# An attention-like mixer and a mixture of experts on one core: sixteen slots, tile steps laced with the mixer's last three steps, setup and scaling moved

## What is computed

```python
h = layernorm(x) * (1 + ca) + sa                      # sa, ca, ga, sb, cb, gb from silu(c) @ wmod, per batch
xi = silu(h @ Win + bin_)                             # 256 columns
# scan over the 512 tokens: state = 0.9 * state + xt * Bp; y = state . Cp + Dp * xt
x = x + ga * (y @ Wout + bout)
h = layernorm(x) * (1 + cb) + sb
p = softmax(h @ Wr + br); probs, idx = top_k(p, 2)    # 8 experts, two per token, renormalised
h_e = layernorm(relu(h @ W1[e] + b1[e]), g1, be1)     # 512 columns
y_e = layernorm(relu(h_e @ W2[e] + b2[e]), g2, be2)   # 128 columns
x = x + gb * sum over the two experts of gate * y_e
```

## Time and profile before

| | |
|---|---|
| median of 3 runs | 551.77 us (550.8 to 551.81) |
| the profiled execution | 549.6 us, its span 547.8 us |
| PE busy (matmuls) | 489.3 us, 89% of the span |
| DVE busy | 472.3 us, 86% |
| ACT busy | 400.9 us, 73% |
| POOL busy | 384.5 us, 70% |
| mean granted clock of PE | 0.969 |

### The profile page before, as it was taken

How to read it: one execution, slowest core, us unless ns; L and a number is a source line. 1 busy time by engine, 2 the same in 40 slices (tenths; PEclk the granted TensorE clock), 3 DMA queues, 4 the chain that set the end, 5 groups by cost and what they waited for, 6 DMA issues and landing times. The chain is left out here.

```text
span 547.8 us, 15172 instructions
## 1 busy us (share of the span) xinstructions
PE 489.3 (89%) x3075; PEld 389.0 (71%) x3075; DVE 472.3 (86%) x2217; ACT 400.9 (73%) x1107; POOL 384.5 (70%) x524
## 2 busy tenths in 40 slices
PE   2698897989896589899999999999999999999863
PEld 2264554555554469699999999999989899889740
DVE  5968899898988578598888899999999899999896
ACT  1435877587876357688888888888888798888763
POOL 4361477777777777866665668888888788769683
PEclk9999999999999589999999999999999999999996
DMA  6962011451111165454555555666666766666665
GB/s 176 309 186 77 31 54 50 95 111 54 55 50 54 55 174 134 136 151 138 143 146 145 173 144 177 179 187 161 182 186 151 181 193 159 184 182 195 189 180 154
DMA packets 79342, 77.81 MB, mean 142 GB/s; under 512 B 11086, under 2 KB 72681, under 8 KB 79126
## 3 DMA queue, kind: packets, MB, share of 16 engines
q1 hardware_dynamic: 70838, 59.92, 42.0%
q0 software_dynamic: 8416, 16.93, 8.7%
HBM read 54.65 MB, written 22.59 MB: 141 GB/s over the span
## 5 line engine op out<-in xcount | busy, mean ns | idle before, releaser
L577 POOL DMA_INDIRECT expert_results<-y,target x135 | 136.3, 1010 | 42.3 <-issue 41.0
L546 POOL DMA_INDIRECT expert_rows<-rows_ring,slot x128 | 123.4, 964 | 54.8 <-issue 53.6
L1344 PE MATMUL bank<-W,h2T 128*128 x1080 | 142.7, 275 | 0.7 <-ACT h2T L727 0.7
L1344 PEld LDWEIGHTS bank<-W,h2T 128*128 128x128 f32 x1080 | 131.2, 192 | 0.9 <-issue 0.9
L719 ACT ACTIVATE h1T<-bank 128x512 f32<-128x512 f32 x135 | 80.7, 598 | 44.6 <-PE bank L1329 43.6
L1108 DVE BATCH_NORM_STATS2 stf<-h1T 128x6 f32<-128x512 f32 x135 | 90.9, 673 | 0.0
L1335 PE MATMUL bank<-ident,h1T 128*128 128x128 f32 x540 | 80.9, 272 | 0.0
L1335 PEld LDWEIGHTS bank<-ident,h1T 128*128 128x128 f32 x540 | 67.3, 141 | 18.2
L727 ACT ACTIVATE h2T<-bank 128x512 f32<-128x512 f32 x135 | 79.6, 589 | 0.0
L1326 PE MATMUL bank<-b_parts,onesr 128*128 x135 | 65.3, 484 | 3.2 <-DVE h3lo L1100 3.2
L1084 DVE SCALAR_TENSOR_TENSOR wmod<-bank,rse,shifts 128x128 f32<-128x128 f32 x135 | 46.5, 344 | 20.5 <-PE bank L1344 7.1
(11 more groups left out here) (212 smaller groups left out, 1037.7 us busy)
## 6 DMA issues: line engine op xcount, KB each, us to landing
shifts<-expert_shifts SPq DMA_DIRECT2D x135, 192.0 KB
hrow<-expert_rows SPq DMA_DIRECT2D x135, 65.0 KB
xi<-expert_results SPq DMA_DIRECT2D x12, 512.0 KB, 5.1
X<-in_L_attn_x SPq DMA_DIRECT2D x8, 512.0 KB, 7.1
out_x<-X SPq DMA_DIRECT2D x15, 256.0 KB
expert_results<-y,target POOLq DMA_INDIRECT x135
shifts<-in_L_ffn_W SPq DMA_DIRECT2D x4, 512.0 KB, 6.4
expert_rows<-rows_ring,slot POOLq DMA_INDIRECT x128, 2.3
```

The costliest lines, as they stand in the source:

```text
L546: nc.gpsimd.indirect_dma_start(out=rows_d, out_offset=bass.IndirectOffsetOnAxis(ap=slot[q][:, n // TOPK, n % TOPK:n % TOPK + 1], axis=0), ...
L577: nc.gpsimd.indirect_dma_start(out=results_d, out_offset=bass.IndirectOffsetOnAxis(ap=target[n % TURN][:], axis=0), in_=y[k][:], in_offset ...
L1344: ins = mm(acc, rT[q][:, ch * P:(ch + 1) * P], W2[:, bass.ds(e2 * CF + ch, 1), :], start=(ch == 0), stop=(ch == CF - 1))
```

## The change

**Slots.** `WIDE_UNTIL = 32`: up to tile 31 results and shifts go round a ring of 16 slots, made of the old eight and of mixer buffers that are free by then (`xi`, `mixT`, `scan`, `spare_gb`); afterwards round eight. Semaphores are shared by pairs of slots. There are 32 `target` tiles. The rows (`hrow`) keep eight slots.

**The seam.** Mixer steps are split in two halves, `mixer_first` and `mixer_second`. The tile steps -1 to 4 stand between the halves of mixer steps 16, 17 and 18 on PE, DVE and ACT. The first tiles get other banks and buffers than the mixer uses (`t3_bank`, `rT_of`). The counts are taken after tile step 5, the second table is made after step 6 and written after step 8, the padding is stored behind the load of tile 15. Round 1 is four batches, 24 tiles. POOL adds shifts between the row stores of batches 14 and 15 (12 tiles) and stores the results afterwards.

**The mixer.** The first statistics and their aggregation are made a step earlier, in pieces between the operations of the Newton chain (`first_stats`, `first_mv`); the second norm is normalised at the end of the step before (in halves); the sums of W2 are made one expert per step in steps 1 to 8; W2 is scaled in steps 11 to 15, seven pieces per step (`scale_w2`).

**The start.** Batch 0 is loaded apart (`first_x_loaded`), the modulation columns are read after its statistics, ACT clears `b1_parts` instead of POOL.

**The gates and the combining.** The Tanh moves to tile step 36; the pieces of batches 0 to 10 are spread evenly over tiles 52 to 132.

The diff, cut to its core:

```diff
-    ROUND1_BATCHES = 3
-    GROUP_ENDS = (ROUND1_BATCHES, 5, 8, 11, 14, 15, 16)
+    ROUND1_BATCHES = 4
+    GROUP_ENDS = (ROUND1_BATCHES, 7, 10, 13, 14, 15, 16)
...
+        FIRST_COMBINED, LAST_COMBINED = 52, EXPERT_TILES - 3
...
+        WIDE_UNTIL = 32
+        xi_flat = [t[:].rearrange("p c l -> p (c l)") for t in xi]
+        y += [xi_flat[0][:, n * D:(n + 1) * D] for n in range(RESULTS)]
...
+        def ring(i):
+
+            return i % (2 * SLOTS) if i < WIDE_UNTIL else i % SLOTS
...
+        SUMS_FROM, W2_FROM, W2_PIECES = 1, 11, 7
...
+        GATED, COUNTED, SPREAD, WRITTEN, OWN_BANKS = 36, 5, 7, 8, 12
+
+        def t3_bank(i):
+
+            return bank[1 + i % 2] if i < OWN_BANKS else bank[6 + i % 2]
...
-            sp.dma_start(X[:, 0:NX, :], x_v[:, 0:NX, :]).then_inc(x_loaded[0], 16)
+            sp.dma_start(X[:, 0:J, :], x_v[:, 0:J, :]).then_inc(first_x_loaded, 16)
...
-                if i >= SLOTS:
-                    sp.wait_ge(y_ready, i + 1 - SLOTS)
...
+                if last_user(i) is not None:
+                    sp.wait_ge(y_ready, last_user(i) + 1)
...
+            for i in range(SLOTS, 2 * SLOTS):
+                load_next(i)
             sp.wait_ge(counts_ready, 1)
...
-            for i in range(SLOTS, ROUND1):
+            for i in range(2 * SLOTS, ROUND1):
                 load_next(i)
...
-            nc.gpsimd.memset(b1_parts[:].bitcast(F32), 0.0).then_inc(pool_consts, 1)
...
+            for n in range(J * TOPK):
+                store_rows((B - 2) % RING, n)
+                if n % 2 == 1:
+                    add_shift(n // 2)
+            rows_of(B - 1)
+            for n in range(J * TOPK):
+                store_rows((B - 1) % RING, n)
+                add_shift(J + n)
...
+            for e in range(E):
+                ins = nc.scalar.activation(b1_parts[:, e, :], padding[:, 0:1].broadcast_to([P, F]), ACT.Copy)
...
-                if on(s - 2, B):
-                    act.wait_ge(nm_ready, s + 2)
-                    normalise(s - 2, n2[q], 0, rs[1 - q], nm[1 - q], n2_ready)
...
+                if on(s - 1, B):
+                    act.wait_ge(nm_ready, s + 3)
+                    normalise(s - 1, n2[1 - q], 0, rs[q], nm[q], range(J // 2))
...
+            run_tiles(expert_step, FIRST2, 1)
+            run(mixer_second, B, B)
+            run_tiles(expert_step, 2, 2)
+            run(mixer_first, B + 1, B + 1)
+            run_tiles(expert_step, 3, 3)
+            run(mixer_second, B + 1, B + 1)
+            run_tiles(expert_step, 4)
...
+            def scale_w2(s, m):
+                n = (s - W2_FROM) * W2_PIECES + m
+                if 0 <= n < E * CF:
...
+                if s == COUNTED + 1:
                     round2_table()
...
+            run_tiles(expert_step, FIRST2, 0)
+            run(mixer_second, B, B)
+            run_tiles(expert_step, 1, 1)
+            run(mixer_first, B + 1, B + 1)
+            run_tiles(expert_step, 2, 2)
+            run(mixer_second, B + 1, B + 1)
+            run_tiles(expert_step, 3, 3)
+            run(mixer_step, B + 2, B + 2)
...
-            def sums_of(experts):
+            def sums_of(e):
...
+            run_tiles(expert_step, FIRST2, FIRST2)
+            run(mixer_first, B, B)
+            run_tiles(expert_step, 0, 1)
+            run(mixer_second, B, B)
+            pe.wait_ge(w2_ready, W2_STEPS)
+            run_tiles(expert_step, 2, 2)
+            run(mixer_first, B + 1, B + 1)
+            run_tiles(expert_step, 3, 3)
+            run(mixer_second, B + 1, B + 1)
+            run_tiles(expert_step, 4, 4)
+            run(mixer_step, B + 2, B + 2)
+            run_tiles(expert_step, 5, COUNTED)
```

More of the change, by code:

```diff
@@ L212, in adaln_ssm_moe_kernel @@
         second_gains = [t[0:E, :] for t in vs[VS - 2:]]
-        target = [sb(f"target_{n}", [P, 1], I32) for n in range(8)]
+        TARGETS = 32
+        target = [sb(f"target_{n}", [P, 1], I32) for n in range(TARGETS)]
         gate = sb("gate", [P, TOPK, NT])
@@ L1120, in expert_step @@
                     ins.then_inc(mve_ready, 1)
-                b = early_batch(s)
-                if b is not None and n % 2 == 1:
-                    early_sum(b, n // 2)
+                for b, j in pieces_at(s - 1):
+                    early_sum(b, j)
                 if s == EXPERT_TILES + 2:
```

483 lines of the change are left out of this document (276 added, 207 removed).

## The result

| | before | after |
|---|---|---|
| median | 551.3 us (4 runs, 547.96 to 551.81) | 563.1 us (4 runs, 561.39 to 564.73) |
| the profiled execution, its span | 549.6, 547.8 us | 564.05, 562.2 us |
| PE busy | 489.3 us | 502.6 us |

A forecast was written before the change was run, and what follows sets the result against it. PE was taken as busy nearly throughout, so only its standing ahead of tile 16 could be won. -6.5 - 6.2 - 9.9 + 2 = -20.6 us gave 529.0 for a like execution, 531 for a median, range 521 to 541.

The forecast's parts named there:

- The steady tile steps, some 110 of them, are untouched by the change: Tile stage from tile 17 on: each step stays at 2.37 us, so the gain lies ahead of tile 16.
- No cost: Tiles 52 to 132: spreading the same 44 combining pieces, pairing semaphores and the ring of 16 were all charged nothing.
- SP's queue becomes the bound of every tile: Rival, tile stage: new waits lengthen SP's cycle from 2.22 to 2.60 us, 27 us over 119 tiles: 558, chance 0.04.
- The start: Up to the first projection: earlier first statistics bring it from 19.88 to 13.4 us, -6.5 us (bounds -4.0 and -7.9).
- The mixer: Mixer steps up to the last matmul of step 15: -6 + 0.8 - 1.5 + 0.5 = -6.2 us.
- The term of steps 0 to 3: First three mixer steps: moved column sums, no wait for the second norm, no late scan on DVE; -6 us.
- The fill-ins: Mixer steps 11 to 15: extra W2 pieces partly hide between dependent DVE operations; about 9.1 us per step, +0.5 in all.
- the rival of 535: Mixer steps 11 to 15: nothing fits between dependent operations, some 0.8 us more per step; 535, chance 0.07.
- The seam: From A, the end of step 15's last matmul, to tile 16's transposition: 61.9 to 52 us, -9.9.
- the seam drags: Rival, between mixer and tiles: late pieces give PE gaps and a 1.2 GHz clock; about 8 us more, 539, chance 0.17.
- The gates: Tile 36: Tanh with two table loads takes 3.0 us of ACT, PE covers about 1.2; +2 us (0 to 3).
- Rival "POOL": POOL's additions wait for late tiles, delaying batch 15's row stores and round 2; PE stands at tile 24; 541, chance 0.03.

The follow-up runs named there:

- own semaphores: The change with one semaphore per shift slot modulo eight for all tiles, instead of pairs: 550.5 us against 550.0 for the kernel before, ratio 1.0024.
- the four repairs: The change with a semaphore per shift slot, pieces every second step, batches 4 and 5 loaded early, gates at tile step 5: 545.1 us against 548.8, ratio 0.9937.

## Why the prediction was wrong

- *"The steady tile steps, some 110 of them, are untouched by the change"*. This is the step that failed, and the largest: with the next item it is 14.7 of the 35.0 us. It also made the difference between no change and slower. I noted that pairs of semaphores "change who waits, not what is done", and left them at nothing. They take a whole tile, 2.3 us, off the lead of every second shift load: the load of the next tile must have landed too. That lead was never measured in the trace of before; SP's and DVE's timelines had it (down to 1.0 us between the load of the next tile's shifts and an even tile's start, where in the change no even tile started under 3.48). 12 us, by one edit alone.
- *"No cost", for the combining.* The pieces cost nothing that shows, but their spacing moved a store onto a load: 2.3 us by the medians beside own semaphores, 3.7 in the traces, and nothing beside the pairs. I had compared the pieces and not what SP issues with them.
- *The rival "SP's queue becomes the bound of every tile"*, 558, chance 0.04, named "result pairs, shift slots in other tiles" and was nearest to what came. Its price was built on a longer SP cycle on all tiles. The cycle did not grow (the shifts of tiles 72 and 73 were issued 2.25 us apart); what grew was how early a load must be issued. That its price came near is luck. It deserved more than 0.04.
- *The start*: right, -7.4 for -6.5.
- *The mixer, -6.2 forecast, +1.3 measured.* The term of steps 0 to 3 failed: I took it to be PE's time, and it is a loop through DVE, ACT and PE. One part is the load of batch 4 (5.11 us of waiting, worth 1.1 when taken away). Another is the second norm in front of `mixT` (2.7 us up to step 3). In these steps DVE's small operations also take 0.56 to 0.67 us instead of 0.17, while POOL splits W1; that this stretches the loop was not tried apart. Steps 3 to 8 are nearly as forecast (9.1 to 9.3 apart, PE busy 9.14 of 9.14 from step 4 to 5). Steps 9 and 10 did not come down to 8.2 (8.94, 8.79). With the load early and the norm late the whole stretch is 146.9 us, -3.0 of the -6.2; the rest stays open.
- *The fill-ins*: right in the main. In the change these steps took 9.3 us on average for the 9.1 forecast. With the norm late, steps with seven W2 pieces take 8.98, the 8.96 of the earlier trace rows with two, so the five more are free in the gaps. The rule of the Trainium skill (page "VectorE: DVE Perf Modes", section "The DRAIN you can't avoid") gave the rival of 535; this case doesn't bear it out for such small operations. The same section also says that an operation which is not held starts earlier, so it does not rule the fill-ins out.
- *The seam, -9.9 forecast, -3.0 measured.* Step 6 came at A + 29.2 instead of A + 24.3. I had DVE as the limit and wrote "hardly a stretch at half clock"; the granted clock was 0.54 for 15 us, PE was busy 13.09 of them, and DVE waited for PE. This is the rival "the seam drags" (chance 0.17). No run holds the clock apart; in the trace of the four repairs the low stretch is shorter (mean 0.88 from A to step 6 instead of 0.77) and step 6 comes at A + 27.3. The padding on SP I had, but only in front of tile 16's rows; the shifts of tiles 12 and 13 stand behind it as well, and through them DVE, ACT and POOL (8.91 us). And a queue that falls back 9 us with 4 to 6 of lead gives it back to nobody: tiles 16 to 24 lost 3.8 more, at a granted clock of 0.92. In the sum for SP, A + 39.1, 1.1 and 9.1 make A + 49.3, not 49.5, which changes nothing.
- *The gates*: +3.7 for +2. The trace has two loads of 1.28 us each, as I took them from the earlier trace rows, and PE was held up by 2.1 us, so the term was right as a wait; what it left out is the granted clock behind the gap, 1.6 us. Two traces of this step at the full clock lost 2.0 and 2.3. The Trainium skill (page "ScalarE: Activation LUTs", section "What ACT_TABLE_LOAD costs") gives about 2.66 us per switch, from which I had +4.5. Its figure is a load and a drain of about 1.38 us behind it; the rows have the load, but the next operation starts 0.02 us behind it (283.48), so the drain is not there. That 3.7 lies between the two sums is chance.
- *Rival "POOL"*, in the changed kernel: no wait for rows at tile 24. It is the next bound, though, as the padding on POOL shows.

## What to carry to other kernels

A semaphore shared by two transfers is a change of the schedule: it makes the first user wait for the second transfer, so before pairing, take the lead of each load over its use from the two timelines and subtract one period. Where work is respaced (here pieces every 1.86 steps), list what every queue issues per tile and look for the places where two large transfers fall together. And a gain ahead of a stage reaches it only if every queue that feeds it (here SP's padding, then POOL's row stores) has that much to spare: look for the bound that keeps its absolute time while the work ahead of it moves.

## What the runs showed of the hardware

- A gap on PE was in part paid twice. The step with the gates lost 2.0 and 2.3 us where the granted clock stayed at 1.00, and 3.7 us where PE, after 1.87 us idle, ran on at the lower level (0.72 over the step). At tile 83 of the change it was the same: 0.81 and 1.10 us idle, a step of 5.36 us at 0.68. What decides between the two was not tried.
- Eight padding stores took SP 8.2 us in a row, POOL 4.3 us in a row right behind the row stores, and some 1.2 us each, with about 0.6 us of idle time before each, where additions came first.
- A shift load of 192 KB was issued at least 3.3 us ahead of DVE's first use in the kernel before, and at least 3.48 us ahead where an even tile waited for the second of a pair in the change (2.7 in the kernel before with pairs). The profile gives a landing for four of these loads:

```profile
spare_gb<-expert_shifts SPq DMA_DIRECT2D x4, 192.0 KB, 3.4
```
